# Ends of the two gate stages cut into feature tiles, in a fused graph and feed-forward kernel

## The reference

```
def _rgcn(x, W_rel, W_root, bias, src, dst, etype):
    xr = jnp.einsum('ni,rio->rno', x, W_rel)
    out = x @ W_root + bias
    for r in range(3):          # mean over the incoming edges of type r
        ...
        out = out + s / jnp.maximum(c, 1.0)[:, None]
    return out

def _gate(h, q, Wg, bg, Wq, bq):          # h: 256 nodes, as 8 batches of 32
    hg = jnp.einsum('bnf,gf->bng', h3, Wg[:, :F])
    qg = jnp.einsum('blf,gf->blg', q, Wg[:, F:]) + bg
    attn = jax.nn.sigmoid(hg[:, :, None, :] + qg[:, None, :, :])
    qi = jnp.einsum('bnlf,blf->bnf', attn, q)
    alpha = jax.nn.sigmoid(h3 @ Wq[:, :F].T + qi @ Wq[:, F:].T + bq)   # shortened
    return alpha * jnp.tanh(qi) + (1.0 - alpha) * h3

h = jax.nn.relu(_rgcn(x, W_rel1, W_root1, b1, src, dst, edge_type))
h = _gate(h, query_embs, Wg, bg, Wq, bq)
h = jax.nn.relu(_rgcn(h, W_rel2, W_root2, b2, src, dst, edge_type))
h = _gate(h, query_embs, Wg, bg, Wq, bq)
```

## Time and profile before

| | |
|---|---|
| Timed executions | 1507.08, 1508.46, 1509.65 us, median 1508.46 |
| Profiled execution | 1502.14 us, its span 1500.4 us |
| PE busy | 1375.5 us, 92% of the span |
| DVE, ACT, POOL busy | 988.2, 772.0, 233.1 us |
| Chain that ended last | PE 74%, DVE 15%, ACT 6%, POOL 3% |
| Mean granted clock of TensorE | 0.957 of 2.4 GHz |

### The profile page before, as it was taken

How to read it: one execution, slowest core, us unless ns; L and a number is a source line. 1 busy time by engine, 2 the same in 40 slices (tenths; PEclk the granted TensorE clock), 3 DMA queues, 4 the chain that set the end, 5 groups by cost and what they waited for, 6 DMA issues and landing times.

```text
span 1500.4 us, 24033 instructions
## 1 busy us (share of the span) xinstructions
PE 1375.5 (92%) x10000; PEld 1166.2 (78%) x10000; DVE 988.2 (66%) x1757; ACT 772.0 (51%) x1240; POOL 233.1 (16%) x119
## 2 busy tenths in 40 slices
PE   6999999799999888798789999889899999988998
PEld 5999633599733577488788899778899999977876
DVE  8645677644677666747668677766577767758455
ACT  2345888434688544444554455634344555436343
POOL 4201576200387400102001000001000000000100
PEclk8999999899999999999999899889899999988899
DMA  8175463125355124034415354063355455132200
GB/s 340 49 226 158 127 190 117 63 96 185 120 160 157 44 68 143 0 126 155 141 44 221 126 179 159 22 232 100 122 189 177 172 190 190 64 138 105 75 0 22
DMA packets 30835, 194.81 MB, mean 130 GB/s; under 512 B 4212, under 2 KB 4340, under 8 KB 14727
## 3 DMA queue, kind: packets, MB, share of 16 engines
q1 hardware_dynamic: 30726, 193.27, 37.5%
HBM read 183.03 MB, written 3.93 MB: 125 GB/s over the span
## 4 chain that ended last, share of the span: by engine, by line
PE 74%; DVE 15%; ACT 6%; POOL 3%; issue 1%; DMA 0%; SPq 0%; DVEq 0%; ACTq 0%
PE PS L357 59%; PE PS L929 6%; PE PS L938 5%; PE PS L362 3%; POOL WK L1117 2%; DVE WL L300 2%; PE PS L609 1%; POOL WL L307 1%; PE PS L459 1%; DVE SM L1284 1%; ACT WH L293 1%; DVE SM L534 1%; DVE WK L1694 1%; ACT WK L1669 1%; DVE XS L484 1%
## 5 line engine op out<-in xcount | busy, mean ns | idle before, releaser
L300 DVE TENSOR_TENSOR WL<-w,WH 128x768 fp32r<-128x768 f32 x363 | 345.4, 963 | 213.1 <-ACT WH L293 210.2
L357 PE MATMUL PS<-XS,WH 128*128 128x256 f32 x2436 | 449.5, 287 | 14.2 <-DVE XS L484 11.4
L293 ACT ACTIVATE WH<-w 128x768 fp32r<-128x768 f32 x381 | 315.8, 841 | 277.7 <-PE PS L357 270.4
L357 PEld LDWEIGHTS PS<-XS,WH 128*128 128x128 f32 x2436 | 383.1, 193 | 18.6 <-issue 10.4
L357 PE MATMUL PS<-XS,WL 128*128 128x256 f32 x1218 | 347.6, 285 | 0.0
L357 PEld LDWEIGHTS PS<-XS,WL 128*128 128x128 f32 x1218 | 234.4, 192 | 0.0
L1059 DVE TENSOR_TENSOR WK<-PS,WK 128x1024 f32<-128x1024 f32 x128 | 156.5, 1223 | 57.5 <-ACT PS L1005 56.6
L1117 POOL TENSOR_TENSOR WK<-WK 128x1024 f32<-128x1024 f32 x64 | 152.9, 2394 | 204.2 <-ACT WK L1002 204.2
L357 PE MATMUL PS<-WH,GS 128*128 128x256 f32 x864 | 163.0, 287 | 6.8 <-DVE GS L484 6.7
L1005 ACT ACTIVATE PS<-PS 128x1024 f32<-128x1024 f32 x128 | 129.4, 1011 | 34.6 <-PE PS L929 34.6
L357 PEld LDWEIGHTS PS<-WH,GS 128*128 128x128 f32 x864 | 137.7, 193 | 9.7 <-DVE GS L484 8.0
(11 more groups left out here) (253 smaller groups left out, 1980.1 us busy)
## 6 DMA issues: line engine op xcount, KB each, us to landing
w<-f2W_in SPq DMA_DIRECT2D x40, 1152.0 KB, 5.4
w<-Wrel_in SPq DMA_DIRECT2D x12, 1152.0 KB, 8.3
WK<-qrep_in SPq DMA_DIRECT2D x16, 768.0 KB, 5.5
w<-f1Wi_in SPq DMA_DIRECT2D x8, 1152.0 KB, 6.3
w<-f1Wo_in SPq DMA_DIRECT2D x8, 1152.0 KB, 5.0
w<-f3Wqkv_in SPq DMA_DIRECT2D x6, 1152.0 KB, 13.5
RT<-qg_rows SPq DMA_DIRECT2D x16, 384.0 KB, 6.3
RT<-AS SPq DMA_DIRECT2D x32, 192.0 KB, 6.6
```

The source lines that it names most:

```text
L293: A.e.activation(w_hi(i), w_raw(i), ACT.Copy).then_inc(*hi("w", i))
L300: V.e.tensor_tensor(w_lo(i), w_raw(i), w_hi(i), ALU.subtract).then_inc(*lo("w", i))
L357: ins = T.e.matmul(o, l, r, start=i == 0 and first, stop=i == n - 1 and last, skip_group_check=lint)
```

## The change

- The `qq` product reads its input from AS, and qiT is split in two parts by nodes: nodes 0 to 223 when the seventh batch is in (`q_in` of a batch moves ahead of the second `weigh` of its step), the last 32 after the last batch. PE waits once, for the second part.
- Each of the six `qq` tiles has its own PSUM bank and its own chain of `pre`, `alpha`, multiplication and addition on 128x256, with one weight tile fed ahead of each of the first five. The lower parts of the last two `qq` tiles are DVE's instead of POOL's. Tanh is ACT's before it feeds them.
- The turns back to node rows are spread: group 0 behind `qq` tile 3, group 1 behind tile 5, group 2 for gate 1 among the aggregates and for gate 2 last. After gate 1 ACT makes all three copies. After gate 2 DVE adds groups 0 and 1 to x, and takes the statistics of group 0, before the chain of tile 5 ends.
- The aggregates of relations 0 and 1 go in the order (r, f) = (0,0) (1,0) (0,2) (1,2) (0,4) (1,4), each behind the copy of its own pair. Relation 0 goes into AS and the split of hT into XS. The order is the same in both rounds.
- The filler matmuls are not changed.

```diff
@@ -60,7 +60,7 @@
...
-                [("qh" + n, "Wqh", None, 6, "V"), ("qq" + n, "Wqq", None, 6, "G")]]
+                [("qh" + n, "Wqh", None, 6, "V"), ("qq" + n, "Wqq", None, 6, "GGGGVV")]]
@@ -92,7 +92,7 @@
...
-                t.pair, t.low, t.end = npair % NPAIR, low, end
+                t.pair, t.low, t.end = npair % NPAIR, low[j % len(low)], end
@@ -742,27 +742,29 @@
...
+        QI = ((0, 224), (224, 256))
...
-        def wait_hN(q, n):
+        def wait_hN(q, n, c):
 
             if n == "1":
                 q.wait_ge(vec, "ln0", 1)
             else:
-                q.wait_ge(act, "hN", 2)
-                q.wait_ge(vec, "hN", 1)
+                q.wait_ge(act, "hN", c)
+
+
+        FIRST_AG = [(0, 0), (1, 0), (0, 2), (1, 2), (0, 4), (1, 4)]
@@ -778,42 +780,60 @@
...
             t0 = FIRST["root" + n]
-            aggregate(0, XSv)
-            aggregate(1, GSv)
+            if n == "2":
+                turn[0] = 3
+            for r, f in FIRST_AG:
+                if n == "2" and (r, f) == (1, 2):
+                    nodes("1", 2)
+                aggregate(r, f)
             bs = [bank(("hid" + n, j), (act, "hid" + n, 2 * j + 1)) for j in range(3)]
-            products(t0, bs, True, False, lambda k: (ASv[:, 0, k, :], ASv[:, 1, k, :]),
-                     lambda k: T.wait_ge(vec, "lower", "x" + n, k - k % 2))
-            products(t0 + 6, bs, False, False, xs_at, lambda k: T.wait_ge(vec, "lower", "ag" + n, 0, k - k % 2))
-            aggregate(2, XSv)
+            products(t0, bs, True, False, xs_at, lambda k: T.wait_ge(vec, "lower", "x" + n, k - k % 2))
+            products(t0 + 6, bs, False, False, as_at, lambda k: T.wait_ge(vec, "lower", "ag" + n, 0, k - k % 2))
+            for f in range(0, 6, 2):
+                aggregate(2, f)
             products(t0 + 12, bs, False, False, gs_at, lambda k: T.wait_ge(vec, "lower", "ag" + n, 1, k - k % 2))
             products(t0 + 18, bs, False, True, xs_at, lambda k: T.wait_ge(vec, "lower", "ag" + n, 2, k - k % 2))
 
...
         def rgcn_act(n):
             t0 = FIRST["root" + n]
...
-            for k in range(0, 6, 2):
...
                 else:
-                    A.wait_ge(vec, "hnew1", 4)
-                act_upper(pair_of(ASv, 0, k), src[:, k:k + 2, :], "x" + n, k)
...
+                    A.wait_ge(vec, "hnew1", k + 1)
+                act_upper(pair_of(XSv, 0, k), src[:, k:k + 2, :], "x" + n, k)
+
+            def aggregate(r, f):
+                A.wait_ge(pe, "ag" + n, r, f)
+                if n == "1" and r == 1:
+                    A.wait_ge(vec, "lower", "qg", 512, 3)
+                act_upper(pair_of(AG_IN[r], 0, f), two(ps("ag" + n, r, f)), "ag" + n, r, f)
+
+            x_in_(0)
+            x_in_(2)
             if n == "1":
-                A.wait_ge(vec, "lower", "qg", 512, 3)
-            aggregate(1, GSv)
+                x_in_(4)
+            for r, f in FIRST_AG:
+                if n == "2" and (r, f) == (1, 2):
+                    nodes_act(2)
+                    x_in_(4)
+                aggregate(r, f)
             act_gemm(t0, 12)
-            A.wait_ge(pe, "w", t0 + 11)
-            aggregate(2, XSv)
+            A.wait_ge(pe, "w", t0 + 5)
+            for f in range(0, 6, 2):
+                aggregate(2, f)
@@ -975,17 +1002,18 @@
...
             turn_q(7)
-            bs = [bank_at(2 + j, ("al" + n, j), (vec, "pre" + n, 2 * j)) for j in range(3)]
+            T.wait_ge(vec, "lower", "qi" + n, 1)
             for f in range(6):
-                o = bs[f // 2][:, (f % 2) * 256:(f % 2) * 256 + 256]
-                T.wait_ge(log, "w", qq_ + f)
+                o = bank_at(2 + f, ("al" + n, f), (vec, "pre" + n, f))
+                T.wait_ge(low(qq_ + f), "w", qq_ + f)
                 wh, wl = w_hi(qq_ + f), w_lo(qq_ + f)
                 for k in range(6):
-                    if f == 0:
-                        T.wait_ge(vec, "lower", "qi" + n, k - k % 2)
                     ks = slice(k * P, (k + 1) * P)
-                    ins = mm(o, three_T(wh[:, ks], wl[:, ks], xs_at(k)), k == 0, k == 5)
+                    ins = mm(o[:, 0:256], three_T(wh[:, ks], wl[:, ks], as_at(k)), k == 0, k == 5)
                 ins.then_inc(*pe("w", qq_ + f))
+                if f == 3:
+                    nodes(n, 0)
+            nodes(n, 1)
@@ -1016,20 +1044,22 @@
...
-            for k in range(0, 6, 2):
-                A.wait_ge(vec, "qi" + n, 7)
-                act_upper(pair_of(XSv, 0, k), qiT[:, k:k + 2, :], "qi" + n, k)
-            feed_act(qq_ + 6)
+            for i, (n0, n1) in enumerate(QI):
+                A.wait_ge(vec, "qi" + n, (6, 7)[i])
+                act_upper(ASv[:, 0, :, n0:n1], qiT[:, :, n0:n1], "qi" + n, i)
             for c in range(0, 6, 2):
-                A.wait_ge(vec, "lower", "qi" + n, c)
                 A.e.activation(tq[:, c:c + 2, :], qiT[:, c:c + 2, :], ACT.Tanh).then_inc(*act("tanh" + n, c))
-            for c in range(0, 6, 2):
-                A.wait_ge(vec, "pre" + n, c)
-                A.e.activation(aT[:, c:c + 2, :], aT[:, c:c + 2, :], ACT.Sigmoid).then_inc(*act("alpha" + n, c))
-                feed_act(nxt + (1, 3, 4)[c // 2])
+            for f in range(6):
+                feed_act((qq_ + 5, qq_ + 6, nxt + 1, nxt + 2, nxt + 3, nxt + 3)[f])
+                if f == 4 and n == "1":
+                    nodes_act(0)
+                A.wait_ge(vec, "pre" + n, f)
+                A.e.activation(aT[:, f, :], aT[:, f, :], ACT.Sigmoid).then_inc(*act("alpha" + n, f))
+            if n == "1":
+                nodes_act(1)
@@ -1074,32 +1104,36 @@
...
+                if p % 4 == 3 and p > 4:
+                    q_in(p // 4 - 1)
                 weigh(p, 2)
...
-                if p % 4 == 3 and p > 4:
-                    q_in(p // 4 - 1)
-            sum_out(7)
-            q_in(7)
-            for k in range(0, 6, 2):
-                vec_lower(pair_of(XSv, 1, k), qiT[:, k:k + 2, :], pair_of(XSv, 0, k), "qi" + n, k)
+            for i, (n0, n1) in enumerate(QI):
+                if i:
+                    sum_out(7)
+                    q_in(7)
+                vec_lower(ASv[:, 1, :, n0:n1], qiT[:, :, n0:n1], ASv[:, 0, :, n0:n1], "qi" + n, i)
...
-            for c in range(0, 6, 2):
-                V.wait_ge(pe, "w", FIRST["qq" + n] + c + 1)
-                V.e.tensor_tensor(aT[:, c:c + 2, :], aT[:, c:c + 2, :], two(ps("al" + n, c // 2)),
-                                  ALU.add).then_inc(*vec("pre" + n, c))
-                qv, hv = tq[:, c:c + 2, :], hT[:, c:c + 2, :]
-                V.wait_ge(act, "alpha" + n, c)
+            for f in range(6):
+                feed_vec((qq_ + 5, qq_ + 6, nxt + 1, nxt + 2, nxt + 3, nxt + 3)[f])
+                if f == 5 and n == "2":
+                    nodes_vec(0)
+                    nodes_stat(0)
+                V.wait_ge(pe, "w", qq_ + f)
+                V.e.tensor_tensor(aT[:, f, :], aT[:, f, :], ps("al" + n, f)[:, 0:256], ALU.add).then_inc(*vec("pre" + n, f))
+                if f == 5 and n == "2":
+                    nodes_vec(1)
+                V.wait_ge(act, "alpha" + n, f)
                 V.wait_ge(vec)
-                V.e.tensor_tensor(qv, qv, aT[:, c:c + 2, :], ALU.mult).then_inc(*vec())
+                V.e.tensor_tensor(tq[:, f, :], tq[:, f, :], aT[:, f, :], ALU.mult).then_inc(*vec())
                 V.wait_ge(vec)
-                V.e.tensor_tensor(hv, hv, qv, ALU.add).then_inc(*vec("hnew" + n, c))
-                feed_vec(nxt + (1, 3, 4)[c // 2])
+                V.e.tensor_tensor(hT[:, f, :], hT[:, f, :], tq[:, f, :], ALU.add).then_inc(*vec("hnew" + n, f))
@@ -1118,16 +1152,29 @@
...
-            feed_pool(qq_ + 6)
-
-        def nodes_pe(n, free):
-            for c in range(3):
-                b = bank(("nd" + n, c), free(c))
-                T.wait_ge(vec, "hnew" + n, 2 * c)
...
+
+        def nodes(n, c):
+
+            b = bank_at(c, ("nd" + n, c), (act, "hN", c) if n == "1" else (vec, "xadd", c))
+            T.wait_ge(vec, "hnew" + n, 2 * c + 1)
+            for m in range(2):
+                for k in range(2):
+                    ins = tr(b[:, m * 256 + k * P:m * 256 + (k + 1) * P], hT[:, 2 * c + k, m * P:(m + 1) * P])
+            ins.then_inc(*pe("nd" + n, c))
+
+        def nodes_act(c):
+            A.wait_ge(pe, "nd1", c)
+            A.wait_ge(act, "tanh1", 4)
+            act_copy(xn3[:, :, c * 256:(c + 1) * 256], ps("nd1", c).rearrange("p (m f) -> p m f", m=2), "hN", c)
+
+        def nodes_vec(c):
+            V.wait_ge(pe, "nd2", c)
+            V.e.tensor_tensor(x3[:, :, c * 256:(c + 1) * 256], x3[:, :, c * 256:(c + 1) * 256],
+                              ps("nd2", c).rearrange("p (m f) -> p m f", m=2), ALU.add).then_inc(*vec("xadd", c))
+
+        def nodes_stat(c):
+            for m in range(2):
+                xstat("f0a", m, c * 256, (c + 1) * 256)
@@ -1137,16 +1184,13 @@
...
-                nodes_pe(n, lambda c: (vec, "xadd", c) if n == "2" else (vec if c == 1 else act, "hN", c))
```

(2 more changed lines are left out.)

71 lines of the change are left out of this document (31 added, 40 removed).

## The result

The changed kernel took 1493.5 us (median of four, 1492.15 to 1495.37), the kernel before beside it 1507.77 (1505.16 to 1509.65): ratio 0.9907, interval 0.9888 to 0.9927. It is faster, as forecast, but the time lies 4.3 us under the predicted 1497.8 and 1.0 us under the range. Each trace is of one execution. That of the changed kernel took 1495.37 us, the slowest of its four; that of the kernel before took 1502.14, quicker than the four beside it. So the spans differ by 6.8 us where the medians differ by 14.3.

The account below looks back on a forecast made before the run. PE was taken to be bound by idling and lower clock at the two gate ends. Gate 1 -10.6, allowance +0.4 and gate 2 -0.5 gave -10.7 us, from 1508.46 to 1497.8 us; 8-in-10 range 1494.5 to 1502.5.

Parts of the forecast that it names:

- the `qq` product of gate 1: Gate 1, PE: the same 108 matmuls take 14.41 us, one lower-clock stretch included; change taken as 0, bounds 1.6 us either way.
- the stages behind gate 2: Behind gate 2: no term in the sum; the forecast counts as wrong if a stage behind 545 us changes length.
- The round: Gate chains: one round of weight tile, `pre`, `alpha`, multiply and add takes 2.59 us on halves, 3.58 on pairs.
- the small split: Gate 1, splitting qiT's last 192 elements: some 0.35 us each on ACT and DVE instead of 0.64 + 0.70.
- Gate 1's sum: Gate 1 up to the root product: -10.6 us, from 0.64 earlier start, 6.97 less waiting and 2.98 of clock.
- the allowance: Gate 1: 0.4 us taken off the gain because both copies of turned rows end close to when PE needs them.
- more is won: Rival, 7%: shorter PE idling ahead of the product keeps 2.4 GHz at one or both gates, -1.6 us each, 1494.6 to 1496.2.
- The filler, not the norms, is late next: Gate 2's end: norms end 3.7 us earlier, but 2.7 of that is lost to the unchanged filler; gate 2 -0.5 us.
- The halves' chain: Rival, 15%, both gates: a half costs what a pair did, rounds take 3.58 us; -2.9 us together, 1505.6 us.
- No weight load took it back: Rival, 4%, downstream: weight loads hold the second round's products, so its end stays; time 1508.0 us.
- The clock did not fall for a whole product: Rival, 4%: turns between `qq` tiles keep the whole product at 1.2 GHz, 11.2 us more at each gate, 1520 us.
- the prediction's own last sign of being wrong: Behind gate 2: the forecast is wrong if a stage behind 545 us changes its length.

Follow-up runs that it names:

- e5: The changed kernel once more with no edit, compared with the kernel before: 1494.28 us, ratio 0.9929.
- e2: The changed kernel with the first group of filler matmuls behind gate 2 cut from 14 to 5: 1486.61 us, ratio 0.9884 to the kernel before.
- e1: The kernel before once more with no edit, compared with the kernel before: 1503.27 us, ratio 0.9984.

## Why the prediction was right in kind and short in size

*What failed, in short.* Three terms: the `qq` product of gate 1, carried at 14.41 us with a stretch of lower clock in it ("I take 0"), took 13.16 without it; the start of the sum, 1508.46 us, lay some 3.7 above what the kernel before took in 62 later runs; and the stages behind gate 2, in the sum at nothing, were 3.4 to 4.7 us longer in both traces of the changed kernel. Why they were is open.

*What bounds, and gate 1's mechanism: right.* The chain of waits at the gate ends was the place. The round was forecast at 2.59 us and is 2.58; the small split at 0.35 on each engine and is 0.36; PE's start at 275.70 and comes at 275.65 (less the 0.28 by which the last sums are late); no idling beyond 0.22 us. The second weight tile of the chain starts at 281.63 on before's scale where 282.62 was forecast, since no lower clock held the tiles ahead of it. The aggregates: 10.02 forecast, 10.19 measured.

*Gate 1's sum: 1.4 us short.* The root product was to start at 301.9 and starts at 300.51 on before's scale, -12.0 us in place of -10.6 (with the allowance, -10.2). Two terms were mis-sized there. The product was carried at 14.41 us, "as PE idles nearly as before ahead of it"; it took 289.46 - 275.93 - 0.37 (the turns in it) = 13.16, without its stretch of lower clock: that was the rival "more is won", priced at 1.6. And each group of turns was carried at its row's 0.60, while from one start to the next they cost 0.37, 0.49 and 0.43: 0.5 less. Against that stand 0.22 of idling and 0.17 in the aggregates. e5, where the stretch did fall into gate 1, has G1 at 222.3, -10.6 against before. So the product's term is a draw between two values, not a constant.

*Gate 2: right in kind, 1.1 us off in the trace.* "The filler, not the norms, is late next" is what happened: the norms end 4.0 us before it (forecast 2 to 3), and cutting it in e2 gave 4.1 us in place (1.3 against e5). But the reading that filler and norms ended together before, 0.11 us apart, took the norm of all nodes: the turn's first half was ready to start at 541.56, so the filler was already the last, by 0.5 us. The last turns were to come 25.13 us behind the last sums and come at 25.40; turns and filler took 12.96 us, forecast 12.1, before 11.51, since the lower clock held for 6.1 us of them, before for 3.1. Hence +0.63 instead of -0.5. In e5 gate 2 gave -2.2. 

*Rivals.* The halves' chain isn't the bound (rounds of 2.58, not 3.58). No weight load took it back: from the root product to the last sums of gate 2 it is 0.38 us less than before. The clock did not fall for a whole product. But the prediction's own last sign of being wrong, a stage behind 545 us that changes its length, did appear: the +4.66 us above, 4.56 of them in one stretch, with more time at 1.2 GHz in it.

*Why the time fell out of the range.* Of the 4.3 us, the larger part is the starting point. The prediction took the change off 1508.46 us, the median of three runs, though its own profiled execution had 1502.14; 62 later runs of the kernel before, in four sessions, have medians of 1504.0 to 1505.4, some 3.7 us lower. From there, -10.7 would have given 1494.0. For the profiled execution itself the prediction had 1491.4, and it came at 1495.37: 4.0 us too low, while the median was 4.3 us too high. So the traces don't explain the miss by mechanism: G1 and G2 together changed by -11.7 us in the first trace and -12.7 in e5 against -10.7, and the tail took back 4.7 and 3.4. That e5's ratio stands for just the forecast -10.7 us is luck in part, as these terms offset each other. The two measured ratios stand for -14.0 and -10.7 us; identical code (e1) moved by 2.4 us. What the range lacked is thus a term of 2 to 3 us for the clock's draws in a kernel that spends 110 us and more of its span at 1.2 GHz.
